# An adaptive-norm FFN and mixture-of-experts layer on one core: the residual rows of x1 turned by VectorE's 32x32 transposes instead of TensorE's

## The reference

```python
x = x + ffn0(cond0(x))      # a 64x64 matrix per sequence, then a 512-2048-512 gated FFN with spline-built weights
# what follows is the second layer; call its input x1
z = x1 @ W.T + scaled low-rank update by the adapter of each sequence
logits = z @ gate_w.T       # 8 experts, the best 2 of them, softmax over the two
out = x1 + sum of the two experts' outputs for z, times their shares
```

## Time and profile before

| | |
|---|---|
| median of 3 runs | 1235.46 us (1233.03 to 1237.46) |
| profiled execution, span | 1234.8 us |
| TensorE busy | 1113.7 us, 90% |
| VectorE busy | 609.1 us, 49% |
| ScalarE busy | 504.3 us, 41% |
| GpSimd busy | 739.4 us, 60% |

### The profile page before, as it was taken

One profiled execution on the slowest core, in us unless ns is written; L12 is line 12 of the kernel. 1 busy time (PEld: TensorE's weight loads), 2 busy tenths in 40 slices (PEclk: granted clock), 3 DMA queues, 4 the chain that ended last, 5 costly groups with the idle time before them and its releaser, 6 DMA issues. The chain is left out here.

```text
span 1234.8 us, 34930 instructions
## 1 busy us (share of the span) xinstructions
PE 1113.7 (90%) x12488; PEld 1033.8 (84%) x12489; DVE 609.1 (49%) x1161; ACT 504.3 (41%) x994; POOL 739.4 (60%) x1083
## 2 busy tenths in 40 slices
PE   2589999999999998788988839999999999999996
PEld 2578998999989998688987839989898989899995
DVE  8846777766777764434434613333333333333332
ACT  3246777776777665344334212222222222222221
POOL 6668898998998986013333424555555545454554
PEclk9869999999999999688989969999999999999999
DMA  6044455554554543733533245475656565744444
GB/s 260 25 128 154 151 207 179 179 184 159 182 202 160 195 135 118 290 133 114 182 115 103 70 143 134 89 205 126 170 123 174 117 180 112 185 73 80 76 76 68
DMA packets 65921, 177.70 MB, mean 144 GB/s; under 512 B 12656, under 2 KB 21752, under 8 KB 62304
## 3 DMA queue, kind: packets, MB, share of 16 engines
q1 hardware_dynamic: 40736, 127.65, 29.6%
q0 software_dynamic: 19200, 38.94, 17.5%
q10 hardware_dynamic: 5952, 10.65, 2.4%
HBM read 105.84 MB, written 71.38 MB: 144 GB/s over the span
## 5 line engine op out<-in xcount | busy, mean ns | idle before, releaser
L1733 POOL TENSOR_TENSOR idle<-small 128x1 f32<-128x1 f32 x284 | 94.7, 333 | 205.6 <-DMA out<-result,scatter_at 106.8
L965 POOL TENSOR_TENSOR in_lo<-inner,in_hi 128x512 fp32r<-128x512 f32 x128 | 175.8, 1374 | 46.3 <-ACT in_hi L1113 46.0
L1807 PE MATMUL banks<-slots,zt_hi 128*128 x568 | 190.6, 335 | 4.8 <-issue 1.7
L1809 PE MATMUL banks<-slots,zt_lo 128*128 x568 | 183.7, 323 | 0.0
L1808 PE MATMUL banks<-slots,zt_hi 128*128 x568 | 182.9, 322 | 0.0
L1201 DVE TENSOR_TENSOR inner<-silu,banks 128x512 f32<-128x512 f32 x128 | 87.6, 684 | 129.4 <-ACT silu L1108 125.9
L1909 DVE TENSOR_TENSOR hid<-silu_g,banks 128x352 f32<-128x352 f32 x71 | 37.0, 521 | 208.3 <-PE banks L1809 208.3
L1756 POOL DMA_INDIRECT out<-result,scatter_at x71 | 113.7, 1601 | 23.9 <-issue 18.8
L1807 PEld LDWEIGHTS banks<-slots,zt_hi 128*128 128x128 f32 x568 | 107.2, 189 | 7.4 <-issue 7.2
L1808 PEld LDWEIGHTS banks<-slots,zt_hi 128*128 128x128 f32 x568 | 107.7, 190 | 0.0
L1108 ACT ACTIVATE silu<-banks 128x512 f32<-128x512 f32 x128 | 76.3, 596 | 76.0 <-PE banks L1034 74.0
(11 more groups left out here) (249 smaller groups left out, 3392.1 us busy)
## 6 DMA issues: line engine op xcount, KB each, us to landing
late_dram<-split_part SPq DMA_DIRECT2D x32, 816.0 KB, 4.3
slots<-late_dram SPq DMA_DIRECT2D x24, 1088.0 KB
raw_part<-in_late_w SPq DMA_DIRECT2D x16, 816.0 KB
x_t<-in_x_t SPq DMA_DIRECT2D x16, 512.0 KB, 3.4
x_both<-in_x_tok SPq DMA_DIRECT2D x16, 512.0 KB, 6.0
x_both<-in_x_res SPq DMA_DIRECT2D x16, 512.0 KB, 3.3
x1t_dram<-x_both SPq DMA_DIRECT2D x16, 512.0 KB, 6.0
x<-x1t_dram SPq DMA_DIRECT2D x16, 512.0 KB
```

The source lines that it names most:

```text
L965: nc.gpsimd.tensor_tensor(in_lo[:, cs, :], inner[u % 2][:, :, :], in_hi[:, cs, :].bitcast(F32), ALU.subtract).then_inc(in_done, 1)
L1733: nc.gpsimd.tensor_tensor(idle[:, at:at + 1], small[:, 0:1], small[:, 0:1], ALU.add)
L1807: nc.tensor.matmul(psum[bank][:, 0:FD], zt_hi[:, k, :], w_high, start=(k == 0), stop=False)
L1809: ins = nc.tensor.matmul(psum[bank][:, 0:FD], zt_lo[:, k, :], w_high, start=False, stop=(k == DK - 1))
```

## The change

TensorE no longer transposes x1, and ScalarE no longer copies the transposed banks. VectorE transposes x1 itself with its transpose instruction, which turns each 32x32 block where it stands: a block of 32 features (partitions) by 32 tokens becomes 32 tokens (partitions) by 32 features, and stays in its group of 32 partitions. So a partition group q holds, for every token, the features of the q-th quarter of each chunk, and a token's row is spread over the four groups. `x1_tok` gets the shape [128, 4 subtiles, 4 token groups, 4 chunks, 32], and the store becomes four DMAs, one for each partition group, which write runs of 128 features (512 B) to the rows. The output's columns stand in another order, which the host undoes at the end, and the experts' down weights are laid out in that order.

```diff
-    out_tiles = out[0:TOK, :].rearrange("(t s p) h -> t p s h", s=LSUB, p=P)
+    out_tiles = out[0:TOK, :].rearrange("(t r n) (q h) -> t q n r h", r=LSUB * QUADS, n=QUAD, q=QUADS)
...
                 def store_out(t):
-                    sp.wait_ge(tok_copied, LSUB * (t + 1))
-                    sp.dma_start(out_tiles[bass.ds(t, 1)].rearrange("a p s h -> p (a s) h"), x1_tok[:, :, :]).then_inc(out_stored, 16)
+                    sp.wait_ge(tok_turned, LSUB * (t + 1))
+                    for q in range(QUADS):
+                        sp.dma_start(out_tiles[bass.ds(t, 1), q:q + 1].rearrange("a q n r h -> n (a q r) h"),
+                                     x1_tok[q * QUAD:(q + 1) * QUAD, :, :, :, :].rearrange("p s a k n -> p (s a) (k n)")).then_inc(out_stored, 16)
                 def next_x1(t):
                     sp.wait_ge(x1t_low, LSUB * t)
+                    sp.wait_ge(tok_turned, LSUB * t)
                     load_x1(sp, t)
...
             def _(pe):
-                def transpose(t, s):
-                    if s == 0:
-                        pe.wait_ge(x1_loaded, 32 * (t + 1))
-                    bank = X1T[s % 2]
-                    pe.wait_ge(drained[bank], use(t, s) + 1)
-                    for k in range(DK):
-                        ins = nc.tensor.transpose(psum[bank][:, k * P:(k + 1) * P], x1[:, k, s * P:(s + 1) * P], ident[:, :])
-                    ins.then_inc(filled[bank], 1)
...
                     for s in range(2):
-                        if has_next:
-                            transpose(t + 1, s)
                         product(t, b, s, 1, range(DK))
...
                     for s in range(2, LSUB):
-                        if has_next:
-                            transpose(t + 1, s)
                         product(t, b, s, 1, range(DK + 1))
...
                     if has_next:
                         for s in range(2):
                             high(t + 1, 1 - b, s)
-                        for s in range(2):
-                            token_rows(t + 1, s)
...
                         if has_next:
                             high(t + 1, 1 - b, s)
-                            token_rows(t + 1, s)
                         copy(t, b, s, 1)
...
+                def turn(t, s):
+                    if s == 0 and not (isinstance(t, int) and t == 0):
+                        dve.wait_ge(out_stored, 16 * QUADS * t)
+                    nc.vector.transpose(x1_tok[:, s, :, :, :].rearrange("p a k n -> p k a n"),
+                                        x1[:, :, s * P:(s + 1) * P].rearrange("p k (a n) -> p k a n", a=QUADS)).then_inc(tok_turned, 1)
...
                         if has_next:
                             low(t + 1, 1 - b, s)
+                            turn(t + 1, s)
...
                 for s in range(LSUB):
                     low(0, 0, s)
+                for s in range(LSUB):
+                    turn(0, s)
                 steps(dve, body)
```

More of the change, by code:

```diff
@@ L70 @@
 TOKP = TOK + P
+QUADS, QUAD = 4, P // 4
 SLOTS = 3
@@ L1261, in adapted_layer @@
         x1t_lo = [sb(f"x1t_lo{b}", [P, DK, LTILE], F32R) for b in range(2)]
-        x1_tok = sb("x1_tok", [P, LSUB, D])
+        x1_tok = sb("x1_tok", [P, LSUB, QUADS, DK, QUAD])
         xa = sb("xa", [P, LTILE])
@@ L1285, in adapted_layer @@
         place_step, counted = sem("place_step"), sem("counted")
-        X1T, XA, RANKS, Z = [0, 1], 2, 3, [[4, 5], [6, 7]]
+        XA, RANKS, Z = 2, 3, [[4, 5], [6, 7]]
         filled = [sem(f"al_filled{i}") for i in range(8)]
@@ L1292, in adapted_layer @@
         x1t_high, x1t_low, xa_split, xa_done, idle_done = (sem(n) for n in ("x1t_high", "x1t_low", "xa_split", "xa_done", "idle_done"))
-        tok_copied, out_stored, early_high = sem("tok_copied"), sem("out_stored"), sem("early_high")
+        tok_turned, out_stored, early_high = sem("tok_turned"), sem("out_stored"), sem("early_high")
         def early_piece(t, e):
@@ L1350, in _ @@
                 steps(sp, body)
-                sp.wait_ge(out_stored, 16 * LNT)
+                sp.wait_ge(out_stored, 16 * QUADS * LNT)
                 for b in range(2):
@@ L1442, in body @@
                             ranks(t)
-                for s in range(LSUB):
-                    transpose(0, s)
                 steps(pe, body)
@@ L1453, in high @@
                     nc.scalar.activation(x1t_hi[b][:, :, s * P:(s + 1) * P], x1[:, :, s * P:(s + 1) * P], ACT.Copy).then_inc(x1t_high, 1)
[L1455 to L1463, removed]
                 def shares(t):
@@ L1520, in _ @@
                     high(0, 0, s)
-                for s in range(LSUB):
-                    token_rows(0, s)
                 steps(act, body)
@@ L1939, with laid_out @@
          "Bm": "L1_cond_Bm", "scalings": "L1_cond_scalings", "router_w": "L1_ffn_gate_w"}
-def laid_out(inputs, columns, gu_window, d_window, tabd):
+def laid_out(inputs, columns, out_columns, gu_window, d_window, tabd):
     x = np.asarray(inputs["x"]).reshape(TOK, D)
@@ L1947, in laid_out @@
     rows = np.zeros((NE, FP, D), np.float32)
-    rows[:, 0:FD] = down.transpose(0, 2, 1)[:, :, columns]
+    rows[:, 0:FD] = down.transpose(0, 2, 1)[:, :, out_columns]
     flat = lambda w, n: w.reshape(NE, n, P, -1).transpose(0, 2, 1, 3).reshape(NE, P, -1)
@@ L1971 @@
     consts, columns, gu_window, d_window, tabd = spline_constants()
-    arrays.update(laid_out(inputs, columns, gu_window, d_window, tabd))
+    out_columns = columns.reshape(DK, QUADS, QUAD).transpose(1, 0, 2).reshape(-1)
+    arrays.update(laid_out(inputs, columns, out_columns, gu_window, d_window, tabd))
     arrays.update(consts)
@@ L1979 @@
     result = run_bass_kernel_spmd(nc, [{f"in_{name}": a for name, a in arrays.items()}], core_ids=[0])
-    return result.results[0]["out"][0:TOK][:, np.argsort(columns)].reshape(BATCH, SEQ, D)
+    return result.results[0]["out"][0:TOK][:, np.argsort(out_columns)].reshape(BATCH, SEQ, D)
```

## The result

The changed kernel takes 1225.55 us (median of 16 executions, 1214.95 to 1231.93), the kernel before 1233.72 us (16 executions in the same rounds, 1225.97 to 1238.97). The ratio is 0.9941, 95% interval 0.9922 to 0.9961: 7.3 us faster by the ratio (8.2 by the medians), where 5.5 us were forecast. The profiled executions span 1228.6 and 1234.8 us.

The account below looks back on a forecast made before the run. The steady middle stage was taken as largely a ring through `ranks`, the indirect DMAs and the release of ScalarE's copy, not TensorE alone. Steady steps 3.6 plus step 0's 1.9 gave 5.5 us off 1235.5: 1230.0 us, range 1217 to 1242.

Parts of the forecast that it names:

- Step 0: First step of the middle stage: products start without transposes, x1's load comes later; 1.9 us won, between -1 and 4.
- the steady steps: Steps 1 to 6 of the middle stage: transpose time saved after ScalarE's copy is released, mainly the fourth group's; 3.6 us.
- the prediction's own sign: Middle stage: the forecast is wrong, on the slower side, if ScalarE waits for the load of x1 beyond step 0.
- The price of a transpose group: TensorE, middle stage: four transposes delay the products by 0.44 us at full clock, 0.85 at the lower clock.
- VectorE's transposes: Middle stage: 32 added 128x512 transposes at 0.68 us, 2.7 us a step, hidden in VectorE's waits.
- the small packets: The store's 2048 runs of 512 B take 4.0 us over 16 engines, against 2.85 for 512 runs of 2 KB.
- the narrow paths: The four stores: a further 1 to 2 us if half the engines' paths serve 32 partitions.
- The slack of the load: x1's load behind the stores has 4.7 us slack; 0 to 1.8 us left after the change, even steps 4 more.
- The rival that was put at 0.10: The store delays the load, so ScalarE's split waits in odd steps; slower, 1254 if 512 B packets cost like 2 KB; chance 0.10.
- The ring: Steady steps: `ranks`, indirect DMAs, copy release, remaining products, next `ranks` set the pace; only TensorE time inside counts, 3.6 us.
- Its other marks: Changed profile: gaps of 5 us in steps 2, 4, 6, 1 to 2 in steps 3, 5; stage 5 to 6 shorter.
- late signal: Late in eight indirect DMAs TensorE's signals reach other engines late; in even steps only at the run's end, gap 4.2 us.

Follow-up runs that it names:

- load_first: The changed kernel with SyncE issuing the load of the next x1 ahead of the four stores; 1197.02 us, 10.9 below the changed kernel.
- wide_stores: The changed kernel with its four 32-partition stores made into four of 128 partitions, same 512 B runs; 1196.5 us.
- after_one_store: The changed kernel with one store of 128 partitions and 2 KB runs, as the kernel before has; 1196.4 us.
- before_again: The kernel before, unedited, run and profiled again where it takes 1206 us instead of 1234; profiled span 1207.3 us.
- after_again: The changed kernel, unedited, run and profiled again where the kernel before takes 1206 us; ratio to the kernel before 1.0009.
- before_four_stores: The kernel before with its one store cut into four of 32 partitions and 512 B runs; 15.3 us slower, ratio 1.0127.

## Why the prediction was right, and where not

**The number.** 1230.0 was forecast and 1225.55 measured, inside 1217 to 1242; a gain of 5.5 us against 7.3. The direction and the size held in the place for which they were made. That the sum came so near is in part luck: two terms missed in opposite directions. Step 0 was to give 1.9 us and lost 0.5 between the profiles' first runs; the steady steps were to give 3.6 and gave 8.2 (steps 1 to 6: 0.6, 0.85, 0.44, 0.85, 0.44 and 0.44 forecast, 0.05, 0.91, 0.49, 2.34, 1.96 and 2.48 measured). And by the prediction's own sign, ScalarE waiting for x1 beyond step 0, its mechanism was wrong on the load already in the result's profile.

**The price of a transpose group** was 0.44 us at the full clock. Where nothing else bounds the stage, it can be read without any model: 19.3 us a step in the kernel before, 17.95 in load_first, wide_stores and after_one_store, so 1.35 us for four groups, 0.34 each. Three groups are worth 0.44; in place of the fourth TensorE has a hitch of its own: in load_first the last matmul ahead of the third product starts at 565.07 and the product's first two at 565.47 and 565.70, where the pitch of 0.12 would have 565.31 for the last, 0.39 us. Steps 0 to 6 together come to the stage's 11.6 us (136.1 to 124.5), near the 12.3 that the prediction gave for all 28 groups, but by another way: step 0 has 3.8 of them, since its first two products no longer wait for the load.

**VectorE's transposes** cost 0.700 us, forecast 0.68, and nothing on the path: after_one_store has them all and runs at TensorE's pace. The indirect DMAs of the stage, some of them beside such transposes, took 994 ns each in the changed kernel and 1007 in the kernel before. By the rule that was named (the Trainium skill, SBUF — State Buffer, Who interferes with whom) they should not disturb each other, and these rows agree.

**Step 0** is the mis-sized term of the sum that can be taken apart. Forecast: load in at 530.6, TensorE on at 532.2, 1.9 us won. In the profile: load used at 532.58, TensorE on at 534.06, nothing won (the first run starts at 549.81, not 549.29; 0.75 us was lost before the stage's first split, so the step itself is 0.2 shorter). The way from the store's issue to the split grew by 2.9 us (8.7 to 11.6), inside the 1.2 to 3 that the prediction allowed. But its parts were the other way round: 1.15 us were given to the small packets and 1 to 2 to the narrow paths, and the runs say 0.1 and 2.5. For step 0 the sum then took 1.4 us of it, where 2.9 came.

**The slack of the load.** "It holds, with 0 to 1.8 us left; in even steps 4 us more" is the step that failed by its argument, on both sides. In the kernel before ScalarE wants x1 11.9 to 12.1 us after the store's issue (before_again, steps 1 to 6; 539.32 to 551.34 in the first), but 10.4 to 11.2 once TensorE is quicker (after_one_store; 530.17 to 541.34 in the first). The prediction's terms had the load in 9.5 to 11.3 us after the issue (7.3, plus 1.2 to 3, plus 1), and behind narrow stores it is in after 11.7 to 14.8 (after_again; 533.47 to 545.20, 590.78 to 605.62). So the change moved the consumer 0.8 to 1.5 us towards the load, which the sum had left out, and the load went further away than the sum's upper end. The 4 us more of even steps were not there even in the profile of the kernel before: the store goes out late in those steps too, and the split stands 12.4, 10.8 and 10.7 us behind it in steps 2, 4 and 6, against 12.0, 13.0 and 13.6 in steps 1, 3 and 5. Accordingly the load is late in the result's own profile by 2.0 and 4.0 us in steps 4 and 6, and by 0.3 in step 5.

**The rival that was put at 0.10**, the store that delays the load, is the one that decides where no signal is late. Its place was right, its packet price wrong (it named 0.055 us a packet; the partitions were the cause), and its size is the difference of after_again and wide_stores, 0.9% or 10 us. In the result's own profile it was at work too, in steps 4 to 6, without turning the sign. The rule of the Trainium skill that spoke for it (DMA: Bandwidth & Descriptors, Rules for kernel authors: 128 partitions and at least 1 MiB in a DMA) is borne out in its first half: 175 against 285 GB/s. Of the second half the runs say less: wide_stores' four DMAs of 256 KB move 285 GB/s against 365 for one of 1 MiB, but with smaller runs too, and have the load in as soon.

**Do the parts add?** The two measures disagree. By the ratios to the kernel before, the transposes off TensorE give -8.6 us (after_one_store) and the narrow stores +15.3 (before_four_stores), together +6.7; the change has +1.1 (after_again, interval -1.4 to +3.5). By the stage they are -11.6 and +10.4, together -1.2, against +0.5. In the stage, then, the narrow stores cost as much without TensorE's transposes (12.1 us, after_again against after_one_store) as with them (10.4), and the parts add to within 2 us of one profile each.

**The ring** (`ranks`, indirect run, release of the copy, rest of the products) fits steps 2 and 3 of the profiles in which it was read, and step 2 best: TensorE goes on 11.86 us after the run's start before and after the change. Its other marks held less. The gaps of steps 2, 4 and 6 were to grow to some 5 us and are 3.95, 4.51 and 3.26 (4.21, 4.43 and 4.54 before), the last of them behind the late load; in steps 3 and 5 ScalarE was to cause gaps of 1 to 2 us, and step 3 has two of 0.6 and 0.7, step 5 none above half a microsecond; the stage is 7.4 us shorter, not 5 to 6. In step 4 TensorE goes on 11.1 us after the run's start instead of 11.8, and the rest of the 2.3 us lies between there and the next run, where less of the stretch ran at the low clock. Before, then after:

```profile
626.04:641.29 15.25, 15.25 (x101) 15.13 (x102) 7.29 (x33) 5.81 (x14) 0.19 (x2) 0.80 0.43 138
624.45:638.02 13.57, 13.57 (x98) 13.44 (x99) 8.54 (x35) 4.94 (x12) 0.19 (x1) 0.87 0.44 98
```

As no experiment met a late signal, the ring could be neither broken nor confirmed. **Open** stays what makes TensorE's signals late there and not here, with the same kernel and the same runs of indirect DMAs, and how the 7.3 us divide between less work on TensorE, shorter gaps, the clock and the store's cost. Whether load_first would gain its 12 us there too wasn't tried.

## What to carry to other kernels

When a change frees the bounding engine, work out the slack of every transfer against the new pace, not the old: here the consumer came 0.8 to 1.5 us nearer, the load went 2.7 us or more further away, and together they ate a gain of 9 to 10 us. Put loads that an engine waits for ahead of stores that nobody waits for; this was worth nothing while the store was quick and 10.9 us once it was slow. And where a profile shows gaps whose releaser is "remote", have a second profile from elsewhere before the whole sum is built on them.

## What the runs showed of the hardware

Four stores of 32 partitions and 512 B runs moved 175 GB/s, the same bytes in the same packets from 128 partitions 285, and one store of 2 KB runs 365. SyncE took 3.4 us in most steps to issue the four narrow ones, 2.1 to 3.7 for the four wide ones and 0.39 for the single one.

VectorE's transpose of 128x512 fp32 took 0.700 us, a group of four 128x128 transposes on TensorE 0.34 us of a step on average, 0.44 where nothing else stands at its place.

The same kernel took 1234 us in one place and 1206 in another, at mean granted clocks of 0.956 and 0.957, and 23.5 of the 27.5 us between the profiled spans lay in the one stage where an engine waits for signals beside runs of indirect DMAs.
